# Windowed attention, MLP and global attention on one core: queues ordered by a walk at build time, and norms by square root and reciprocal

## The reference

```
qn = q / jnp.clip(jnp.linalg.norm(q, axis=-1, keepdims=True), 1e-12)
kn = k / jnp.clip(jnp.linalg.norm(k, axis=-1, keepdims=True), 1e-12)
attn = jnp.einsum('bhnd,bhmd->bhnm', qn, kn) * scale
attn = jax.nn.softmax(attn + bias[None], axis=-1)
out = jnp.einsum('bhnm,bhmd->bhnd', attn, v)
...
h = jax.nn.relu(_group_norm(x + h, gn1_w, gn1_b, GROUPS))
m = _group_norm(h, mlp_gn_w, mlp_gn_b, GROUPS)
m = jax.nn.relu(jnp.einsum('bchw,ec->behw', m, mlp_w1) + mlp_b1[None, :, None, None])
m = jnp.einsum('behw,ce->bchw', m, mlp_w2) + mlp_b2[None, :, None, None]
z = jax.nn.relu(_group_norm(h + m, gn2_w, gn2_b, GROUPS))
```

```
attn = jax.nn.softmax(jnp.einsum('bhdn,bhdm->bhnm', q, k) * scale, axis=-1)
out = jnp.einsum('bhnm,bhdm->bhdn', attn, v).reshape(b, c, h, w)
return jnp.einsum('oc,bchw->bohw', w_proj, out) + x
```

## Time and profile before

| | us |
|---|---|
| median of 3 runs | 13579.03 |
| lowest, highest | 13576.19, 13617.23 |
| the profiled execution: its time | 13596.65 |
| its span | 13594.8 |
| PE, DVE, ACT, POOL busy | 10259.9, 7793.6, 6665.1, 2866.9 |
| mean granted clock of PE | 0.878 of full speed |

### The profile page before, as it was taken

How to read it: one execution, slowest core, us unless ns; L and a number is a source line. 1 busy time by engine, 2 the same in 40 slices (tenths; PEclk the granted TensorE clock), 3 DMA queues, 4 the chain that set the end, 5 groups by cost and what they waited for, 6 DMA issues and landing times.

```text
span 13594.8 us, 221286 instructions
## 1 busy us (share of the span) xinstructions
PE 10259.9 (75%) x69254; PEld 3810.3 (28%) x69254; DVE 7793.6 (57%) x10100; ACT 6665.1 (49%) x14018; POOL 2866.9 (21%) x786
## 2 busy tenths in 40 slices
PE   3589586895858958588585886958779586795898
PEld 1233232332323323233232322323223232332332
DVE  2366464664646646466464665646556465674675
ACT  0146354563545635356363553635546354463576
POOL 6310403104040040401304013040220403104000
PEclk9598798997979979799797988979889798997899
DMA  0101001010010200102011020110101001010010
GB/s 17 24 6 20 15 14 21 6 22 14 13 22 6 31 6 14 20 6 31 5 16 19 5 31 6 17 18 7 29 6 19 16 8 28 6 21 15 13 20 13
DMA packets 108484, 213.65 MB, mean 16 GB/s; under 512 B 52438, under 2 KB 84118, under 8 KB 107162
## 3 DMA queue, kind: packets, MB, share of 16 engines
q1 hardware_dynamic: 107298, 198.50, 9.1%
HBM read 65.75 MB, written 41.47 MB: 8 GB/s over the span
## 4 chain that ended last, share of the span: by engine, by line
PE 57%; POOL 16%; DVE 14%; issue 7%; DMA 2%; SPq 2%; ACT 1%; DVEq 0%; ACTq 0%; POOLq 0%
PE PS L1128 17%; PE PS L1117 15%; POOL tok_h L580 15%; PE PS L983 11%; DVE small L765 9%; PE PS L1024 3%; PE PS L1042 2%; DMA x_in<-in_x 2%; PE PS L1072 2%; PE PS L1080 1%; PE PS L1032 1%; DVE small L798 1%; SPq L485 1%; PE PS L1088 1%; DVE small L809 1%
## 5 line engine op out<-in xcount | busy, mean ns | idle before, releaser
L692 ACT ACTIVATE exps<-PS 128x392 f32<-128x392 f32 x12800 | 5875.0, 497 | 6455.3 <-PE PS L1117 6310.3
L765 DVE TENSOR_REDUCE small<-PS 128x1 f32<-128x784 f32 x6400 | 5934.9, 968 | 2274.1 <-PE PS L983 2268.9
L1117 PE MATMUL PS<-q_stack,k_stack 99*128 99x392 bf16 x12800 | 3879.7, 348 | 67.3 <-issue 41.7
L983 PE MATMUL PS<-k_stack,q_stack 96*128 96x392 bf16 x12800 | 3271.9, 343 | 539.8 <-DVE small L765 503.7
L1128 PE MATMUL PS<-exps,v_all 128*32 128x392 f32 x25600 | 2962.8, 536 | 4.4 <-ACT exps L692 4.4
L1117 PEld LDWEIGHTS PS<-q_stack,k_stack 99*128 99x128 bf16 x12800 | 1185.0, 99 | 3418.8 <-ACT exps L692 2448.7
L580 POOL TENSOR_TENSOR tok_h<-tok_h,vec 128x784 f32<-128x784 f32 x16 | 2003.7, 125233 | 136.0 <-DVE tok_h L786 136.0
L983 PEld LDWEIGHTS PS<-k_stack,q_stack 96*128 96x128 bf16 x12800 | 1166.9, 101 | 1667.9 <-DVE small L765 971.3
L1014 PE MATMUL PS<-tok_h,w_spread 128*128 128x392 f32 x256 | 120.0, 601 | 1989.4 <-POOL tok_h L580 1981.0
L790 DVE SCALAR_TENSOR_TENSOR tok_unit<-tok_qk,vec,PS 128x784 f32<-128x784 f32 x64 | 66.0, 1031 | 2045.1 <-PE PS L1014 2045.1
L598 POOL TENSOR_TENSOR win_scores<-win_scores,small 128x784 f32<-128x784 f32 x256 | 384.1, 1501 | 3858.3 <-DVE small L810 3858.3
(11 more groups left out here) (98 smaller groups left out, 4825.0 us busy)
## 6 DMA issues: line engine op xcount, KB each, us to landing
q_stack<-tok_qk SPq DMA_DIRECT2D x320, 98.0 KB, 3.9
k_stack<-tok_qk SPq DMA_DIRECT2D x320, 98.0 KB, 4.2
kmask<-tok_unit SPq DMA_DIRECT2D x1024, 12.2 KB
scratch_att<-o_st SPq DMA_DIRECT2D x512, 26.0 KB
att<-scratch_att SPq DMA_DIRECT2D x33, 392.0 KB
z_half<-scratch_z SPq DMA_DIRECT2D x33, 392.0 KB, 11.4
inv_sums<-scratch_rden SPq DMA_DIRECT2D x132, 98.0 KB, 3.2
out<-inv_sums SPq DMA_DIRECT2D x33, 392.0 KB, 3.7
```

The lines of the kernel that those rows point to most:

```text
L692: nc.scalar.activation(exps(u), PS[:, u % SCORE_BANKS, 0:GTOK], ACT.Exp, scale=D1 ** -0.5).then_inc(s_exps, 1)
L765: nc.vector.tensor_reduce(max_parts[:, n_:n_ + 1], slot(), op=ALU.max, axis=AX.XY)\
L983: last = mm(PS[:, it.bank + j, 0:GTOK], q_stack[0:STACK, stage // 2, tile * 128:(tile + 1) * 128], k_stack[0:STACK, stage // 2, chunk * GT ...
L1117: mm(PS[:, u % SCORE_BANKS, 0:GTOK], k_stack[0:STACK + SHIFT, h, kt * 128:(kt + 1) * 128], q_stack[0:STACK + SHIFT, h, c * GTOK:(c + 1) * ...
```

## The change

**The order.** The hand-set times, the shares and the common list go. `PARTS` lists for each step which engines it uses in turn and how long each takes, in units of 10 ns. `layer0_needs`, `finish_needs`, `attention_needs` and `maxima_needs` list what each step waits for. `arrange` walks all engines together at build time: each in turn takes, of the steps that are ready, the one of best rank (on PE shift, then other steps of slots, then maxima, then scores and weighing), and notes it. Each engine gets its own list. Maxima may not run ahead of two a quad; layer 0's PE steps have an earliest quad (`earliest_unit`), with groups 10 quads apart from quad 20 on. In PE's queue a weighing now stands after three scores of the next quad, as before; the other steps may stand between any two. SP and POOL, DVE and ACT too, no longer follow one list: SP now has `sums` and `zload` ahead of all `xload`s, and `rspread` ahead of the last two; POOL has `scale` ahead of all squares; PE has `final` of the older half at quad 7 (before: quad 13) and of the younger at quad 184 (before: 188).

**The norms.** All eight chunks' head sums go to one bank: the second four chunks use weights shifted by 16 rows and add to the first four. So 392 columns remain, ACT takes their square root, DVE the reciprocal, and POOL does no power of that size. `w_head_sum` and `w_spread` get a second variant, with ten more weight loads.

**Smaller.** `piece_l` goes from DVE to POOL, and what was a step `rest` of its own now belongs to `gqk`.

```diff
+PARTS = {
+    "score": (("PE", 17),), "exp": (("ACT", 41),), "weigh": (("PE", 86),),
+    "max": (("PE", 34), ("DVE", 90)), "shift": (("PE", 25), ("DVE", 16), ("SP", 25)),
...
+    "norms": (("ACT", 310), ("DVE", 250)), "spread": (("PE", 140), ("DVE", 96)),
+    "kload": (("SP", 60),), "queries": (("SP", 8),), "twice": (("POOL", 85),),
...
+    "stack": (("SP", 90),), "vcopy": (("POOL", 60),),
...
+TAIL = {"PE": 20, "DVE": 18, "ACT": 18, "POOL": 15, "SP": 350}
+STACK_TAIL = 900
...
+MAX_START, MAX_RATE = 1, 2.0
...
+    while left:
+        engine = min(ENGINES, key=lambda e: free[e])
+        now, best, soon = free[engine], None, []
+        for n, (since, step, part) in enumerate(offered[engine]):
+            kind = step.kind
+            if engine == "PE" and kind in SLOTS:
+                if len(slots) >= 2:
+                    if slots[-2] not in emptied:
+                        continue
+                    since = max(since, emptied[slots[-2]])
...
+                rank = {"shift": 0, "max": 2}.get(kind, 1)
...
+            else:
+                rank = 1 if engine == "DVE" and kind not in SLOTS else 0
...
-                elif it.kind == "sum":
-                    pl.wait_ge(s_sums_bounded, t + 1)
-                    nc.gpsimd.tensor_tensor(tok_h[:, 0:PAIR], tok_h[:, 0:PAIR],
-                                            minus_half.broadcast_to([128, PAIR]), ALU.pow).then_inc(s_norms_inverted, 1)
...
+                elif it.kind == "norms":
+                    act.wait_ge(s_sums_bounded, t + 1)
+                    nc.scalar.activation(tok_h[:, 0:GTOK], tok_h[:, 0:GTOK], ACT.Sqrt).then_inc(s_norms, 1)
...
+                elif it.kind == "norms":
+                    dve.wait_ge(s_norms, t + 1)
+                    nc.vector.reciprocal(tok_h[:, 0:GTOK], tok_h[:, 0:GTOK]).then_inc(s_norms_inverted, 1)
...
-                            last = mm(PS[32 * j:32 * j + 32, it.bank + r, 0:GTOK], w_head_sum[:],
-                                      tok_h[:, g * GTOK:(g + 1) * GTOK], start=True, stop=True)
+                            last = mm(PS[32 * j:32 * j + 32, it.bank, 0:GTOK], w_head_sum[:, r, :],
+                                      tok_h[:, g * GTOK:(g + 1) * GTOK], start=(r == 0), stop=(r == 1))
```

More of the change, by code:

```diff
@@ L41 @@
 STAGE_MAXIMA = [[m for m in MAXIMA if m[0] == stage] for stage in range(STAGES)]
[L43 to L55 removed]
+LEAD = 6
@@ L57, in layer0, with at, all_of, layer0_needs @@
+LEAD_IN = STAGE_MAXIMA[0] + STAGE_MAXIMA[1][:LEAD]
+Step = namedtuple("Step", "kind i j k")
+Entry = namedtuple("Entry", "kind i j k part bank")
+def at(kind, i=0, j=0, k=0):
+    return Step(kind, i, j, k)
+def all_of(kind, count):
+    return [at(kind, n) for n in range(count)]
+def layer0_needs(attended):
+    needs = {}
+    def step(this, *before):
+        needs[this] = [b if isinstance(b, tuple) and not isinstance(b, Step) else (b, None) for b in before]
     for g in range(GROUPS):
-        put(1 + 0.8 * g, "xload", g)
@@ L59, in layer0 @@
-        put(2.5 + 0.8 * g, "xorder", g)
+        step(at("xload", g), *([at("xorder", g - 2)] if g >= 2 else []))
+        step(at("xorder", g), at("xload", g))
     for i in range(4):
-        put(8 + i, "qk", i)
-        put(16.5 + i, "spread", i)
-    put(14.5, "sum")
-    first, period = 22, 8
+        step(at("qk", i), at("xorder", 2 * i + 1), *([at("stack", 3)] if attended else []))
+        step(at("spread", i), at("norms"))
+    step(at("sum"), *all_of("qk", 4))
+    step(at("norms"), at("sum"))
@@ new lines, in layer0_needs @@
+    group_norm(1, *all_of("hstats", 4))
+    for c in range(GROUPS):
+        step(at("mlp1", c), at("mlp_in", c // 2), *([(at("mlp2", c - 2), 0)] if c >= 2 else []))
+        step(at("mlp2", c), at("mlp1", c))
+    group_norm(2, *all_of("mlp2", GROUPS))
+    step(at("zstore"), *all_of("zrelu", 4))
+    for k in range(3):
+        step(at("gv", k), *all_of("zrelu", 4))
+    for h in range(3):
+        left = [at("weigh", (2 * h + 2) * TILES - 1)] if attended else []
+        step(at("stack", h), *all_of("piece_l", 4), *left)
+        step(at("vcopy", h), *all_of("gv", 3), *left)
@@ new lines, in maxima_needs @@
+def maxima_needs(maxima, stages):
+    needs = {at("max", *m): [] for m in maxima}
+    for n, stage in enumerate(stages):
+        needs[at("shift", stage)] = [(at("max", *STAGE_MAXIMA[stage][-1]), None)]
+        if n:
+            needs[at("shift", stage)].append((at("shift", stages[n - 1]), None))
+        first = at("max", *STAGE_MAXIMA[stage][0])
+        if stage in (0, 6) and first in needs:
+            needs[first].append((at("stack", stage // 2 if stage == 0 else 3), None))
+    return needs
```

463 lines of the change are left out of this document (242 added, 221 removed).

## The result

| | before | after |
|---|---|---|
| median, us (4 runs each, same chip) | 13598.13 | 10824.75 |
| lowest, highest | 13576.19, 13633.13 | 10812.4, 10869.28 |
| the profiled execution's time; its span | 13596.65; 13594.8 | 10812.4; 10810.6 |
| mean granted clock of PE | 0.878 | 0.950 |

The ratio of the medians is 0.796, with a 95% interval of 0.793 to 0.800: 20% less time. 10950 was forecast, with a range of 10400 to 11600.

What follows compares the result with a forecast made beforehand. It took PE's wait for POOL's power (15% of the span) as first bound, then PE and the order. 15 loop images at -166.8 us and -139 for the prologue took 13596.65 to 10956, stated as 10950 us; range 10400 to 11600.

Steps and rivals of the forecast that it cites:

- The power, -124 an image: POOL's power turning head sums into inverse norms: PE's wait for it goes, 123.8 us an image.
- Root and reciprocal, +3: ACT's root with two table loads and DVE's reciprocal push exponentials and maxima: 3 us an image on PE, between 0 and 6.
- The order, -65: Window groups, the quads behind them and quads 16 to 23 lose less waiting: 65 us an image, bounds 0 and 95.
- -5 of the sum: Quads 16 to 23 lost 6 us an image before; five of that come back.
- 32+19: Gains an image: 32 us in the eight window groups, 19 in quads 86 to 123 behind them.
- The end, +9: Younger half's final product, 8 to 9 quads behind the copy: PE waits 9 us an image for the chain copy to scale.
- The start, +10: Image start: PE waits 7 us for x at quad 5 and 8 at quad 7's final product, less 5 lost before.
- The prologue, -139: Before the loop images: -124 for the power, -24 for the order of eight groups, +5 weight loads, +4 norms.
- The last image, 0: Image without layer-0 work: an earlier final product may wait, maxima are spread; no change.
- A: Rival: the order packs nearly as well as meant and DMA chains cost half; 10350 us, chance 0.22.
- B: Rival: the power goes, the order gives nothing and DMA chains cost double; 12220 us, with part gain 11300 to 12200, chance 0.18.

Runs made afterwards that it cites:

- experiment 1: The kernel before with its old hand-set order and only the norms of the change (root on ACT, reciprocal on DVE): 11640 us, ratio 0.8569.
- experiment 2: The changed kernel with the norms as one power on POOL over 392 columns, placed by the walk, instead of root and reciprocal: 10982 us, ratio 0.8093.
- experiment 3: The changed kernel with the square root replaced by a plain copy on ACT, so no table is loaded inside the images: 10764 us, ratio 0.7931.
- experiment 4: The changed kernel with the earliest quads of the two final products moved from 8 and 185 to 14 and 190: 10704 us, ratio 0.7875.
- experiment 6: The changed kernel with later final products and the image's start laid out anew: 10613 us; a further step with the first qk at quad 11: 10392 us.
- experiment 7: The changed kernel with maxima ranked behind scores right after a weighing or maximum: 10779 us; a variant on the mended start: 10517 us.
- e10_qk_later: Mended start plus maxima rule, with first qk at quad 11 instead of 8, spreads and final product at 18: 10392 us against 10517 without these moves.
- e3_x_first: The changed kernel with x loads ahead of sums, zload and rspread on SP, and the sums' reciprocal not before quads 5 and 179: 10924 us, ratio 0.8036.
- e8_start_mended: The changed kernel with final products at 17 and 190, stack transfers behind two x loads, reciprocal, scale and first qk later: 10613 us, ratio 0.7814.

## Why the prediction was right

The mechanism was right: the stall behind the power was worth what its wait said, the order packed the groups about as forecast, and the waits that the table brought stood where they were forecast. The time came out 1% under the forecast. The terms follow, by the starts of the weighings, as means over the 15 loop images of the profiled executions, set against the norms alone.

**The power, -124 an image.** Shown by experiment 1: with root and reciprocal in its place a loop image is 122.4 us shorter, the prologue 120.8 (the sum had -123.8 +3 = -120.8, and -124 +5 +4 = -115). That the gain is one of place, not of POOL's work, the prediction took from the waits; experiment 2 bears it out, with the power at half its width.

**Root and reciprocal, +3.** 3.1 us of ACT, 2.6 of DVE, 2.3 of wait on PE; 3 to 4 us by experiment 3.

**The order, -65.** Quads 24 to 149 take 425.8 us instead of 492.7: -67, where the sum has -60. Quads 16 to 23 take 24.6 instead of 31.5: -7 for the -5 of the sum. Groups of 10 quads take 32.7 us (33 to 34 were forecast), at a clock of 1.00. The old groups of 8 quads took 33.0, so nearly the same time now has two more quads in it. The parts came out less well than their sum: in quads 24 to 149 the time at the lower clock, worked out from the granted clock, fell from 59 to 13 us, which is worth about 23 us by an estimate (half of it) where the prediction had 9, and time multiplied by clock fell by 44 where it had 32+19. Which part of the new order gives this, the groups' period, the ranks or the engines' own lists, no run separates.

**The end, +9.** Quads 150 to 199 take 137.2 us instead of 127.6: +9.6, and experiment 4 takes 9.7 of it away by moving the final product alone.

**The start, +10.** Quads 0 to 15 take 72.8 us instead of 62.7: +10.1. **This step had the place right and the resource wrong, and its size is luck**: the prediction had waits of 7 us for x and 8 for scale; they have 2.1 us each. It looked at SP's queue and at PE's readers, and did not see that DVE has the reciprocal of the sums in front of its maxima and waits 7 us for a load that is itself behind the stack; PE waits 6.0 us for that. Nor did it count the clock here: in quads 0 to 9 the time at the lower level is 21 us instead of 7. These ten quads cost 17.3 us more than with the norms alone, and quads 10 to 15, which gave work to them, 7.2 less.

**The prologue, -139.** The first weighing is at 371.1 instead of 529.1 us: -158, of which the power has 121 and the order 37 instead of 24.

**The last image, 0.** The miss: +22 us (494.4 instead of 472.3). The prediction set "an earlier final product may wait" against "maxima are spread" and wrote 0. Quads 0 to 9 of the last image take 45.0 us instead of 26.5, and from quad 175 to the last weighing it is 61.3 instead of 56.9; what lies between is 0.6 us shorter. So the waits cost all of it: the ends of the two halves stand there, with no layer-0 work beside them. Experiment 4 takes 19.5 us away, experiment 6 leaves no long quad. The maxima won nothing, and one reason is the walk's full quad, 0.09 us above the old one: experiment 7 wins 12 us in quads 10 to 174. That the walk would change the full quad the prediction did not look at: it took 2.24 us over from the earlier trace rows.

The sum against the measurement, by the trace: 15 x -176.5 -158 +22 = -2784, the difference of the spans. Forecast was 15 x -166.8 -139 = -2641. The 143 us that were too few are 9.7 us an image (7 in quads 24 to 149, 2 in quads 16 to 23, 1.6 in the power, less 0.7 at the start and the end) and 19 in the prologue, less the last image's 22.

**The rivals.** A asked for 625 us an image or less and B for 720 or more; it was 660. Part of A was to be had: e10_qk_later has 636 us an image and 10392 us, 4% under the changed kernel, with other numbers in its pace and two other rules of rank.

## What to carry to other kernels

Before you shorten a slow instruction, look at which queue has its reader and how far behind: here a power of 63 us, half as wide, cost 7 us an image once its reader stood late enough, and one of 125 us had cost 122. When a planner sets the order, its result is as good as its durations for transfers: compare each first reader of a transfer with the time at which the trace shows it landed, on every engine, not on the bound one alone, and check what the planner does to the most frequent quad, since a tenth of a microsecond there is paid in every one. Of two waits remove the one that the busy engine meets first, but judge by the whole stretch with its clock, since a moved wait can cost more than the old one. And before you credit an edit with a few microseconds, compare a stretch that it left alone: here one and the same queue of 64 quads took 222.3 us in one kernel's images and 228.4 in another's, by the clock alone.

## What the hardware showed that I had not expected

- In e3_x_first the granted clock fell to the 1.2 GHz level 2 us behind a wait of 1.8 us on PE and stayed there for 41 us, with one more wait of 4.1 us inside and PE busy throughout for the last 32. In the changed kernel it was 10 us, around the end of a wait of 6.0 us. What decides the length was not settled.
- Two table loads around a square root took 1.28 us each, with no gap to the exponentials on either side.
- The power on POOL took 62.9 us for 392 columns and 125.2 us for 784: 160 ns a column at either width. The reciprocal on DVE took 2.59 us for 392, as the 6.15 ns an element of the earlier trace rows say.
- The first x loads, issued ahead of the stack's twelve transfers (at 1654.23 us in e8_start_mended), were read by POOL only at 1668.93, 14.7 us later, and from 1655 to 1667 us the DMA engines were busy throughout, at 141 GB/s. So the stack's place ahead of them in SP's queue is not what made them late here. The loads of att and z were issued just before them; whether those or the stack's transfers held them, no run separates.
